# The stack of K parts filled through a scratch in DRAM, by 12 transfers a batch in place of 24 within SBUF

## The reference

```
k = (ctx @ Wk.T + bk).reshape(32, 1601, 16, 16)        # 16 heads of 16
v = (ctx @ Wv.T + bv).reshape(32, 1601, 16, 16)
q = (layernorm(x) @ Wq.T + bq).reshape(32, 64, 16, 16)
score = einsum('bqhd,bkhd->bhqk', q, k) / sqrt(16)
score = score + where(qmask & kmask, 0, -1e18)
x = x + einsum('bhqk,bkhd->bqhd', softmax(score), v)
```

## Time and profile before

| | |
|---|---|
| median of 3 runs | 1871.67 us (1859.99 to 1872.77) |
| the profiled execution | 1864.99 us, span 1863.1 us |
| PE busy | 1528.9 us, 82% of the span |
| DVE, ACT, POOL busy | 1149.6, 922.5, 914.8 us |
| granted clock of TensorE, mean | 0.899 |
| DMA queue of SP | 150.52 MB, 30.9% of 16 engines |

### The profile page before, as it was taken

One profiled execution on the slowest core, in us unless ns is written; L12 is line 12 of the kernel. 1 busy time (PEld: TensorE's weight loads), 2 busy tenths in 40 slices (PEclk: granted clock), 3 DMA queues, 4 the chain that ended last, 5 costly groups with the idle time before them and its releaser, 6 DMA issues. The chain is left out here.

```text
span 1863.1 us, 59544 instructions
## 1 busy us (share of the span) xinstructions
PE 1528.9 (82%) x24355; PEld 1041.6 (56%) x24355; DVE 1149.6 (62%) x1778; ACT 922.5 (50%) x1191; POOL 914.8 (49%) x611
## 2 busy tenths in 40 slices
PE   2789999999999999999999999999967686069107
PEld 0456666666666666666666666666643575034006
DVE  6655655565555656565565655566653896966885
ACT  1245555455555555555555556555552344336741
POOL 6366565444656545465654556564205455750320
PEclk9889999999999999999999999999979698579558
DMA  5533343433334343333444333343216000100001
GB/s 162 124 107 91 98 122 99 133 92 91 91 100 121 97 133 93 91 92 99 120 104 130 91 91 96 101 122 99 56 47 136 1 0 1 51 1 1 0 0 46
DMA packets 84232, 155.16 MB, mean 83 GB/s; under 512 B 15320, under 2 KB 47832, under 8 KB 84000
## 3 DMA queue, kind: packets, MB, share of 16 engines
q1 hardware_dynamic: 82640, 150.52, 30.9%
q10 hardware_dynamic: 1360, 0.98, 0.2%
HBM read 61.08 MB, written 2.20 MB: 34 GB/s over the span
## 5 line engine op out<-in xcount | busy, mean ns | idle before, releaser
L619 DVE TENSOR_REDUCE MXP<-W_PS 128x1 f32<-128x512 f32 x768 | 502.9, 688 | 314.3 <-PE W_PS L455 314.3
L540 ACT ACTIVATE PR<-S_PS 128x1024 f32<-128x1024 f32 (+1 forms) x416 | 425.9, 1024 | 325.5 <-PE S_PS L405 324.2
L352 POOL TENSOR_TENSOR K_HI<-K,MCOL 128x512 f16<-128x512 f32 (+1 forms) x224 | 217.0, 969 | 520.4 <-ACT K L548 520.4
L405 PE MATMUL S_PS<-QS,STK 105*128 105x128 f16 (+1 forms) x3328 | 268.0, 225 | 54.0 <-issue 46.6
L354 POOL TENSOR_TENSOR K_LO<-K,K_HI 128x512 f16<-128x512 f32 (+1 forms) x224 | 275.0, 1228 | 17.6
L455 PE MATMUL W_PS<-STK,QS 105*128 105x512 f16 (+1 forms) x1024 | 269.1, 334 | 6.5 <-DVE MXP L619 5.2
L418 PE MATMUL O_PS<-PR,V 128*17 128x64 f32 x13312 | 266.7, 220 | 1.2 <-ACT PR L540 1.1
L418 PEld LDWEIGHTS O_PS<-PR,V 128*17 128x17 f32 x13312 | 194.5, 97 | 126.2 <-issue 87.0
L405 PEld LDWEIGHTS S_PS<-QS,STK 105*128 105x128 f16 (+1 forms) x3328 | 198.7, 101 | 96.5 <-issue 48.7
L438 PE MATMUL W_PS<-WV_HI,CTX_HI 128*128 128x256 f16 (+1 forms) x832 | 237.4, 285 | 4.5 <-DVE WV_LO L597 3.5
L438 PE MATMUL W_PS<-WV_LO,CTX_HI 128*128 128x256 f16 (+1 forms) x832 | 236.4, 284 | 0.0
(11 more groups left out here) (218 smaller groups left out, 1929.7 us busy)
## 6 DMA issues: line engine op xcount, KB each, us to landing
CTX<-in_ctx_t SPq DMA_DIRECT2D x64, 800.5 KB, 5.7
STK<-K_HI SPq DMA_DIRECT2D x256, 128.0 KB, 2.6
STK<-K_HI SPq DMA_DIRECT2D x256, 72.1 KB, 2.1
STK<-K_LO SPq DMA_DIRECT2D x128, 128.0 KB, 2.7
STK<-K_LO SPq DMA_DIRECT2D x128, 72.1 KB, 2.1
QSTK<-STK SPq DMA_DIRECT2D x12, 192.0 KB, 3.9
X<-in_x SPq DMA_DIRECT2D x1, 2048.0 KB, 19.0
SK<-QK_HI SPq DMA_DIRECT2D x8, 256.0 KB, 5.0
```

Source lines behind the costliest of these rows:

```text
L352: pool.tensor_tensor(K_HI[:, m, lo:hi], k32, zero, ALU.add).then_inc(k_hi, 1)
L405: last = pe.matmul(S_PS[par][0:m, j * 2 * SQ:(j + 1) * 2 * SQ], STK[u][0:KROWS, j, i * P:i * P + m], QS[0:KROWS, u, j, :, :], start=True, ...
L540: nc.scalar.activation(PR[0:m, par, :], S_PS[par][0:m, :], ACT.Exp).then_inc(p_sb, 1)
L619: dve.tensor_reduce(MXP[:, j, at:at + 1], bank[:, :], AX.X, ALU.max).then_inc(mx_done, 1)
```

## The change

K_HI and K_LO are no longer read by the fills. A new step, keep, writes each half of both parts to a scratch in DRAM, k_parts (two batches x 2 parts x 256 features x 1601 tokens), by one transfer each: 4 a batch, of 512 KB for half 0 and 289 KB for half 1. The fills then read from the scratch: for each half, for each of 2 groups of 4 neighbouring pairs, 3 transfers into 32 partitions each, 256 KB for half 0 and 144 KB for half 1, 12 a batch in place of 24. They wait for the writes to land (k_out) in place of k_lo. POOL's wait before it overwrites K_HI is now for the writes and no longer for the fills. mx_part follows the groups: MX 0 to 7 belong to pairs 0 to 3, MX 8 to 15 to pairs 4 to 7, MX 16 to 19 and 20 to 23 likewise. SP's program per body becomes the fill of b+1, the load of b+3, and then keep of b+2, half 0 and half 1.

```diff
 def mx_part(i):
     if i < A_MX:
-        return i // 4, [(i // 4 + 4 * (i % 4 // 2), 0)], i % 2
+        return i // 8, [(i // 2, 0)], i % 2
     if i < 24:
-        return i % 8 // 2, [(i % 8 // 2 + 4 * (i % 2), 0)], 2
+        return i % 8 // 4, [(i % 8, 0)], 2
...
+        def keep(n, u, half):
+
+            lo, hi = (0, HALF) if half == 0 else (HALF, LK)
+            sp.wait_ge(k_lo, PER["K"] * n + (4 if half == 0 else 7))
+            for q, part in enumerate((K_HI, K_LO)):
+                sp.dma_start(dram["k_parts"][u, q, :, lo:hi].rearrange("(m p) t -> p m t", p=P), part[:, :, lo:hi])\
+                    .then_inc(k_out[half], 16)
+
         def stack(n, u, half):
             lo, hi = (0, HALF) if half == 0 else (HALF, LK)
-            done = stk_a if half == 0 else stk_b
             if half == 0:
                 need(sp, s_ps, NT * (n - 1))
-            sp.wait_ge(k_lo, PER["K"] * n + (4 if half == 0 else 7))
-            if half == 0:
                 sp.dma_start(STK[u][ROW_MASK:ROW_MASK + 1, :, :],
...
-            for c in range(4):
-                rows = slice(32 * c, 32 * c + 32)
-                for q, part in enumerate((K_HI, K_LO, K_HI)):
-                    sp.dma_start(STK[u][32 * q:32 * q + 32, c::4, lo:hi], part[rows, :, lo:hi]).then_inc(done[c], 16)
+            sp.wait_ge(k_out[half], 32 * (n + 1))
+            for c in range(2):
+                for q, part in enumerate((0, 1, 0)):
+                    sp.dma_start(STK[u][32 * q:32 * q + 32, 4 * c:4 * c + 4, lo:hi],
+                                 dram["k_parts"][u, part, P * c:P * c + P, lo:hi].rearrange("(j d) t -> d j t", d=32))\
+                        .then_inc(stk[half][c], 16)
...
+        keep(0, 0, 0)
+        keep(0, 0, 1)
         stack(0, 0, 0)
...
         load(2)
+        keep(1, 1, 0)
+        keep(1, 1, 1)
...
             if prepare:
                 stack(b + 1, 1 - u, 0)
                 stack(b + 1, 1 - u, 1)
             if fetch:
                 load(b + 3)
+            if ahead:
+                keep(b + 2, u, 0)
+                keep(b + 2, u, 1)
...
             if i == 0:
-                for c in range(4):
-                    need(pool, stk_a[c], 48 * n)
+                need(pool, k_out[0], 32 * n)
             elif i == 4:
-                for c in range(4):
-                    need(pool, stk_b[c], 48 * n)
+                need(pool, k_out[1], 32 * n)
...
-                    if i < A_MX and i % 4 == 0:
-                        pe.wait_ge(stk_a[c], 48 * (n + 1))
-                    elif A_MX <= i < 24 and i % 2 == 0:
-                        pe.wait_ge(stk_b[c], 48 * (n + 1))
+                    if i < A_MX and i % 8 == 0:
+                        pe.wait_ge(stk[0][c], 48 * (n + 1))
+                    elif A_MX <= i < 24 and i % 4 == 0:
+                        pe.wait_ge(stk[1][c], 48 * (n + 1))
```

## The result

The changed kernel takes 2067.78 us in the median (2063.76 to 2077.19, 4 runs) against 1868.99 us before (4 runs): ratio 1.108, 95% interval 1.102 to 1.114. The forecast was 2026 us, between 1970 and 2105. The direction and the mechanism of the long waits were right; the size was 157 us forecast against 199 us measured.

What follows compares the result with a forecast made beforehand. TensorE (PE), busy 82%, was taken to set the pace. 18 batches x (6.0 us idle + 2.6 us slower clock) = 155 us on 1864.99, plus 7 to the median: 2026 us (+8.3%), range 1970 to 2105.

Steps and rivals of the forecast that it cites:

- The path: On SP, the next stack's fill stands behind the wait for K_LO 6; 7.7 us from there to MX 0.
- The long waits: PE before MX 0 in 18 batches without a jump back: idle 6.0 us each, ends 4.3 and 10.
- the SK rows: Self-attention transfers of 256 KB into 32 partitions: first lands after 3.3 us, then one every 1.27; used to price the fills.
- The clock: After each long wait PE's clock falls to half, adding 2.6 us per batch, ends 0 and 2.8.
- the 12 batches with a jump back: MX 0 comes 8.5 us after K_LO 6 there, so the 7.7 us path fits: cost 0.
- a sign that it would be wrong: The forecast said it would be wrong if the 12 batches with a jump back wait for the stack too.
- SP's own jump back: SP's possible pause at its loop jump, now on the path in 12 batches: 0 to 4 us, taken as 0.
- The rate: Fills into 32 partitions stay near half of 384 GB/s even from DRAM, since the written side limits them.
- The low case: If the read side set the rate, fills from DRAM would go at 384 GB/s, idle near the low end, 4.3 us.
- Costed at nothing: Half-0 landing in DRAM, context loads, later groups and second half, added traffic and prologue: all taken as 0.
- Hidden: Rival: the stack lands before PE asks for it, time 1872 us; chance 0.03.
- faster: Rival: with fills gone from PE's jump back, its pause shrinks to about 2.5 us, clock stays up; 1823 us, chance 0.02.

Runs made afterwards that it cites:

- the order experiment: Changed kernel with SP's write of half 1 moved behind the fill of half 0; 1896.85 us, ratio 1.018 to the kernel before.
- the same order without DRAM: Kernel before, with the fill of half 0 waiting for all 7 units of K_LO in place of 4; 1918.06 us, ratio 1.030.

## Why the prediction was right, and where it was off

- **The path, right.** "K_LO 6, keep half 1, mask row, three transfers, MX 0" is what SP's rows show; the order experiment removes five sixths of the loss, and the same order without DRAM costs 3%.
- **The long waits, right in number, 12% short in size.** 18 were forecast and 18 came, 6.84 us on average in place of 6.0. In the batch shown, issue was 1.96 us where I took 1.7, and the three transfers took 6.3 us where the SK rows and 0.2 gave 6.0; it waited 6.44 us, the average one 0.4 longer. That is 18 x 0.8 = 15 us of what the sum lacked.
- **The clock, right in size for these waits.** 2.6 us forecast; PE's busy time grew by 2.5 a batch over the 18. As a constant it was wrong: the table has 0.9 to 2.5 us for waits of 2.0 to 6.8.
- **The mis-sized term, and the step that failed: the 12 batches with a jump back, priced at 0 and measured at 31 us**, three quarters of the 42 us by which the sum was short. The forecast named their waiting as a sign that it would be wrong, and that sign came. It set a path of 7.7 us against 8.5 us until MX 0. In the body shown the path was 8.66 us (868.10 - 859.44), and PE came for MX 0 at 866.52, 7.1 us after K_LO 6: its pause was 3.45 us in place of 3.96, and the clock was back at 1.00 by 864, 4.4 us after PE had started again, in place of 5.6. Over the 12 the path was 9.2 us, and all of them waited, 1.0 to 2.9 us. Two numbers within 0.8 us of each other were treated as a safe order, and the 8.5 came from one body: in the kernel before the 12 have 6.8 to 8.6 us there, 8.1 in the mean, two of them less than the forecast's own path.
- **SP's own jump back, right.** From the second write of half 1 to the mask row: 0.74 us in a batch without a jump (813.24 to 813.98), 1.02 with one (859.87 to 860.89). 0.3 us, not 4.
- **The rate, right.** With 256 KB into 32 partitions from DRAM it was 218 GB/s with full engines, 199 from SBUF. The low case that needed 384 GB/s did not come. The rule on ports of the Trainium skill, "SBUF — State Buffer", section "Door 1: The DMA port swizzle", by which 32 written partitions bound the rate, agrees with these rows, in which the source hardly matters.
- **Costed at nothing, right:** the landing of half 0 in DRAM (hidden here, some 4.6 to 6.7 us from the first issue when uncovered), context loads (landing after 11.1 us and in time), the second half (no wait at MX 16), the prologue but for 1.9 us in body 0, of which 0.9 are a wait for STK.
- **The rivals.** "Hidden" and "faster" are refuted by the 31 waits. But the effect that "faster" built on exists: with the DMA engines 0.06 to 0.08 busy during the pauses at the jumps in place of 0.66 to 0.89, the pauses were 3.5 us in the mean in place of 3.9, and 3.5 with the same order within SBUF too, whose batches behind a jump came out 1.1 us shorter (4.1 forecast). In the changed kernel that gain became waiting for the stack. That the free engines are the cause was not isolated. In this order 24 transfers beat 12 by 100 us, since the first consumer waits for three of them. The coalescing rule of the Trainium skill, "DMA: Bandwidth & Descriptors", section "Rules for kernel authors", gives overhead under 64 KB as its reason; transfers of 128 KB already had the rate of the larger ones here, so there was nothing to gain by it, and it was not borne out.

## What to carry to other kernels

Larger transfers that do not raise the rate delay their first consumer; before merging transfers, look which of them is waited for first. In a queue that issues in order, a wait put at the end of a body stands ahead of everything of the next body: ask of each new wait what is queued behind it. A wait of some us on TensorE costs more than its length, and a neighbouring pause can hide a path or another wait until somebody removes the pause. Before an effect on top is read off a total, split the total by kinds of batches: here a gain in 12 of them hid a loss in 18. And where a forecast rests on one length being shorter than another, read both in more than one body.

## What the runs showed of the hardware

- A DMA write of 512 KB from SBUF to DRAM, the second of two, lands after 4.1 us in the median, and a fill that waits for both started 4.8 us after the first was issued in the body shown, 4.6 us in most others without a jump and 5.8 to 6.7 behind one.
- SP issues a transfer from DRAM into 32 partitions every 0.49 us and a write to DRAM in 0.36 to 0.47 us, where those within SBUF take 0.64.
- PE's busy time grew by 0.9 us behind waits of 2.0 us, 1.7 behind 3.0, 2.0 behind 4.2 and 2.5 behind 6.8; the clock fell behind idle stretches of 1.73 us in 5 of 12 batches.
- 24 useless matmuls in each of 17 waits took 34 us off PE's other busy time in them; the kernel became 2.6% faster, in part from batches that they did not touch.
- Code written out in full removed the 12 pauses of PE of 3.9 us but gained 45 us in place of 83: in even bodies that no pause precedes a DVE cast takes 4.47 us in place of 0.77 beside a POOL instruction, and PE waits 1.73 us for DVE. In odd bodies the same cast beside the same instruction takes 0.74 us; why was not settled.
